# An adaLN block on one core: the transposes of the probabilities ahead of the value product

## The chip, the core and the metric

The kernel runs on one core of a Trainium2 chip. The metric is the device time of one execution, in microseconds (us). Five engines work side by side, each through its own list of instructions in order, and tell each other by semaphores when something is done: TensorE (PE in the profile, with its weight loads as PEld), VectorE (DVE), ScalarE (ACT), GpSimd (POOL) and the queue of SyncE (SP), which only starts transfers here. TensorE writes to PSUM, from where ScalarE and VectorE take its results; GpSimd works on SBUF alone.

## What is computed

A transformer block with adaptive layer norm, in float32. Two sequences of 1024 rows with 512 features; 32 query heads of 128 features share 8 key/value heads, four to one; a row attends to itself and the 127 before it. Cut to what matters:

```python
h = _layernorm(x) * (1 + ca) + sa
q, k, v = rope(h @ wq), rope(h @ wk), h @ wv
scores = jnp.einsum('bqhgd,bshd->bhgqs', qg, k) * sm_scale
allowed = (j <= i) & (j > i - SLIDING_WINDOW)
attn = jax.nn.softmax(jnp.where(allowed, scores, neg), axis=-1)
out = jnp.einsum('bhgqs,bshd->bqhgd', attn, v).reshape(B, S, N_Q_HEADS * HEAD_DIM)
x = x + ga * (out @ wo)
h = _layernorm(x) * (1 + cb) + sb
x12 = h @ w12.T + b12                       # split into x1 and x2
x = x + gb * ((silu(x1) * x2) @ w3.T + b3)
```

## The kernel before

**Units and heads.** Attention is cut into units: one key/value head with its four query heads (`G`), one tile of 128 rows of the sequence. A head has eight units, for the eight tiles of a sequence (`NT`), and there are 2 sequences with 8 heads, so 128 units. All engines walk through them in step: step u of a head starts unit u, and at the same time carries unit u-1 and unit u-2 on. The words "step 5" below mean the step that starts a head's unit 5. The loop body holds eight steps (2 to 9, where 8 and 9 are steps 0 and 1 of the next head); the first two steps and the last head of each sequence are written out behind and ahead of it by the same functions.

**Precision.** Each product is made of three matmuls (`mm3`, lines 275, 276 and 277), of the rounded part (hi) and the rest (lo) of both operands: hi by hi, hi by lo, lo by hi. So every result that TensorE consumes again is split in two: ScalarE rounds it (hi), VectorE subtracts that from the original (lo).

**The way of a unit.** `scores` (PE, 12 matmuls of 192 columns into the PSUM tile `pS`); `merge` (DVE: lines 853, 856, 859; the maximum, and `nb` from it); `exps` (ACT, line 613, into `pr`); `recip` (DVE, line 864); `normalise` (POOL, line 1193, on `pr`); then in the next step `trans` (PE, line 285: four transposes of `pr` into the PSUM tile `pTr`), `p_hi` (ACT, line 606) and `p_lo` (DVE, line 839) from `pTr` into `pT`, and `mask` (POOL, line 1186: four selects from `pT` into `pm`, two for the first unit of a head); in the step after that `p_times_v` (PE: six matmuls of 512 columns from `pm` and the values into the PSUM tile `pAv`, three for a first unit), `result_hi` (ACT, line 601) and `result_lo` (DVE, line 834) from `pAv` into `oT`, and `out_proj` (PE: 12 matmuls of 512 columns into `pOp`), which DVE adds to `y` (`add_y`, line 898). There is one `pT`, one `pm`, one `pAv` and one `oT`: `mask` of a unit waits until `p_times_v` of the unit before has read `pm`; `trans` and `p_hi` wait for the unit before too.

**What fills the rest of a step.** Between those stand the projections of the next half head ("jobs"): one or two projections in a step (12 matmuls of 512 columns each, into `pP`), with their rope: `swap` on ACT (lines 623, 624), `rope_cos` (869), `rope_sum` (875) and `rope_lo` (886) on DVE, `rope_sin` (1199) on POOL. DVE and ACT also split the weights that arrive (`split_weight`, lines 996 and 596; in steps 2, 3, 4 and 5), and in steps 4 to 6 a row tile of the other layer norm goes through ("side": `side_stats`, `side_apply` on DVE, `side_rstd` on POOL, line 1216, `side_transpose` on PE, line 383).

**What sets the order.** It is written out by hand: each engine has its own `unit_step`, which calls the functions above in one fixed order. On PE before: `scores(u)`, `p_times_v(u-2)`, `trans(u-1)`, the jobs, `out_proj(u-2)`, and what is late. On ACT: `result_hi(u-2)`, `p_hi(u-1)`, `exps(u)`, jobs. On DVE: `merge(u)`, `result_lo(u-2)`, `p_lo(u-1)`, the jobs with `recip(u)` among them, the splits, `add_y(u-2)`. On POOL: `mask(u-1)`, `normalise(u)`, the jobs' `rope_sin`, and in step 4 `side_rstd`. `mask` waits for `u_plo` of its own unit and `u_av` of the one before.

Of the kernel before, what the change touches and what calls it, by code (L numbers as in the profile page):

```python
# [71 lines left out]
def adaln_block(nc, x, wq, wk, wv, wo, w12, b12, w3, b3, cond, wmod, cos, sin, x1_spill, out):  # L72
# [13 lines left out]
    with ExitStack() as ctx:  # L86
# [114 lines left out]
        def window(a, hp):  # L201

            return 512 * a + 256 * hp
# [5 lines left out]
        def blocks(q, part):  # L209

            return q[:, part].rearrange("p h q -> p (h q)").rearrange("p (t h q) -> p t h q", t=2 * CH, h=G)
# [60 lines left out]
        def _(pe):  # L272
            def mm3(o, hi_l, lo_l, hi_r, lo_r, start, stop):

                nc.tensor.matmul(o, hi_l, hi_r, start=start, stop=False, skip_group_check=True)  # L275
                nc.tensor.matmul(o, hi_l, lo_r, start=False, stop=False, skip_group_check=True)  # L276
                return nc.tensor.matmul(o, lo_l, hi_r, start=False, stop=stop, skip_group_check=True)  # L277

            def trans(f, u):

                f.wait(u_norm, PER_U, u + 1)
                f.wait(u_phi, PER_U, u)
                f.wait(u_plo, PER_U, u)
                for i in range(G):
                    last = nc.tensor.transpose(  # L285
                        pTr[:].rearrange("p (h a q) -> p a h q", h=G, a=2)[:, i // 2, 2 * (i % 2):2 * (i % 2) + 2, :],
                        pr[:, u % 2, i, :], ident[:].rearrange("p (h q) -> p h q", h=2))
                last.then_inc(u_trans, 1)

            def scores(f, u, b):  # L290
                t = u % NT

                f.wait(j_done, PER_J, JB - 1 + (6 if t >= CH else 0) + PER_J * (u // NT))
                f.wait(u_exp, PER_U, u)
                q = qT[t // CH]
                for a in range(2):
                    lo = 0 if t else P - 64 * a
                    ks = slice(t * P - P + 64 * a + lo, t * P + 64 * a + 64)
                    for hp in range(2):
                        at = window(a, hp)  # L300
                        q_hi, q_lo = (blocks(q, i)[:, 2 * (t % CH) + a, 2 * hp:2 * hp + 2, :].rearrange(
                            "p h q -> p (h q)") for i in range(2))
                        last = mm3(pS[:, at + lo:at + 192], q_hi, q_lo, kv[:, 0, 0, ks], kv[:, 1, 0, ks], True, True)
                last.then_inc(u_scores, 1)

            def p_times_v(f, u, b):

                t = u % NT
                f.wait(u_mask, PER_U, u + 1)

                f.wait(j_done, PER_J, JB + (6 if t >= CH else 0) + PER_J * (u // NT))

                for own in ((1, 0) if t else (0,)):
                    tt = t - own
                    v_hi, v_lo = (kv[:, i, 1, tt * P:(tt + 1) * P] for i in range(2))
                    last = mm3(pAv[:], v_hi, v_lo, pm[:, own, 0].rearrange("p h q -> p (h q)"),
                               pm[:, own, 1].rearrange("p h q -> p (h q)"), own == 1 or t == 0, own == 0)
                last.then_inc(u_av, 1)
# [86 lines left out]
            def unit_step(f, u, b, jobs, late=lambda: None, prev=True, prev2=True):  # L405

                scores(f, u, b)
                if prev2:
                    p_times_v(f, u - 2, b if u >= 2 else b - 1)
                if prev:  # L410
                    trans(f, u - 1)
                jobs()
                if prev2:
                    out_proj(f, u - 2)
                late()
# [64 lines left out]
            for b in range(B):  # L480
                s0 = b * NKV
                f = Frame(pe, s0)
# [17 lines left out]
                with nc.tensor.Fori(s0, s0 + NKV - 1) as s:  # L500
                    f = Frame(pe, s, regs, s0)
                    for u in range(2, NT + 2):
                        unit_step(f, u, b, lambda: slot_jobs(f, u, b), lambda: slot_late(f, u, b))
                f = Frame(pe, s0 + NKV - 1)
# [87 lines left out]
        def _(act):  # L592
            def split_weight(f, dst, W, slot):

                f.wait(w_in[slot], 32, 16 * (W // 5 + 1))
                nc.scalar.copy(dst, st[:, slot, :]).then_inc(w_hi, 1)
# [6 lines left out]
            def p_hi(f, u):  # L603
                f.wait(u_trans, PER_U, u + 1)
                f.wait(u_mask, PER_U, u)
                nc.scalar.copy(pT[:, 0].rearrange("p h q -> p (h q)"), pTr[:]).then_inc(u_phi, 1)
# [95 lines left out]
            def splits(f, u, b):  # L702

                for k, dst in weight_pieces(u):
                    if k >= 10:
                        f.wait(j_pe, PER_J, JB + k - 10 + 1)
                    split_weight(f, dst[0], k, k % 5)

            def unit_step(f, u, b, jobs, prev=True, prev2=True, split=True):
                if u == 2:  # L710

                    f.wait(u_scores, PER_U, u + 1)
                    splits(f, u, b)
                if prev2:
                    result_hi(f, u - 2)
                if prev:
                    p_hi(f, u - 1)
                exps(f, u)
                jobs()
                if split and u in (3, 4, 5):  # L720
                    splits(f, u, b)
# [46 lines left out]
            for b in range(B):  # L768
                s0 = b * NKV
                f = Frame(act, s0)  # L770
# [12 lines left out]
                with nc.scalar.Fori(s0, s0 + NKV - 1) as s:  # L783
                    f = Frame(act, s, regs, s0)
# [4 lines left out]
                f = Frame(act, s0 + NKV - 1)  # L789
# [41 lines left out]
        def _(dve):  # L831
# [5 lines left out]
            def p_lo(f, u):  # L837
                f.wait(u_phi, PER_U, u + 1)
                nc.vector.tensor_tensor(pT[:, 1].rearrange("p h q -> p (h q)"), pTr[:],  # L839
                                        pT[:, 0].rearrange("p h q -> p (h q)"), ALU.subtract).then_inc(u_plo, 1)  # L840
# [157 lines left out]
            def splits(f, u):  # L998
                for k, dst in weight_pieces(u):
                    split_weight(f, dst, k, k % 5)  # L1000

            def unit_step(f, u, b, jobs, late=lambda: None, prev=True, prev2=True, split=True):
                merge(f, u)
                if u == 2:
                    splits(f, u)
                if prev2:
                    result_lo(f, u - 2)
                if prev:
                    p_lo(f, u - 1)
                jobs(lambda: recip(f, u))  # L1010
                if u == 4:
                    side_stats(f)
                if split and u in (3, 4, 5):
                    splits(f, u)
                if prev2:
                    b2 = b if u >= 2 else b - 1
                    add_y(f, u - 2, b2)
                if u == 4:
                    side_apply(f)
                if u == 6:  # L1020
                    side_lo(f)
                late()
# [63 lines left out]
            for b in range(B):  # L1086
                s0 = b * NKV
                f = Frame(dve, s0)
# [14 lines left out]
                with nc.vector.Fori(s0, s0 + NKV - 1) as s:  # L1103
                    f = Frame(dve, s, regs, s0)
# [3 lines left out]
                f = Frame(dve, s0 + NKV - 1)  # L1108
# [406 lines left out]
```

## Time and profile before

| | us |
|---|---|
| median of three runs | 1521.19 |
| lowest and highest of them | 1519.98, 1522.48 |
| the profiled execution, its own time | 1520.32 |
| its span, from the first to the last instruction | 1518.4 |
| TensorE busy | 1485.9 (98% of the span) |
| TensorE weight loads | 1229.1 (81%) |
| VectorE busy | 1100.7 (72%) |
| GpSimd busy | 865.4 (57%) |
| ScalarE busy | 830.5 (55%) |

A row of the timeline gives the start in us, the time taken in us, the engine, the line of the kernel, the operation, what is written and read, and how many instructions stand in the row. In brackets is idle time of the engine before it and who ended it. Matmuls overlap, so that their durations say little; the distance from one start to the next is what a matmul costs.

### The profile page before, as it was taken

What the parts mean: (1) busy time and instruction counts of PE and PEld (TensorE: products, weight loads), DVE (VectorE), ACT (ScalarE), POOL (GpSimd) and SP (SyncE); (2) the same over time, 40 slices, a digit from 0 to 9 for tenths busy, and PEclk for the clock granted to TensorE, in tenths of its full rate; (3) what the DMA queues carried; (4) which work ended last, traced back from release to release, by engine and by line L of the source; (5) the groups of instructions that cost most, each with busy time, mean ns of one, the idle gap of its engine ahead of it and who ended that gap; (6) DMA issues with size and microseconds to landing.
All of it is one profiled execution on the core that took longest, in us unless ns stands there. A gap on an engine that the chain in (4) does not pass through costs nothing.

```text
span 1518.4 us, 27309 instructions
## 1 busy us (share of the span) xinstructions
PE 1485.9 (98%) x7561; PEld 1229.1 (81%) x7561; DVE 1100.7 (72%) x1844; ACT 830.5 (55%) x2195; POOL 865.4 (57%) x892
## 2 busy tenths in 40 slices
PE   7899999999999999999999999999999999979998
PEld 3478888888888888887888888888888888868887
DVE  5578787878787878788787878787878778753542
ACT  3565565555555656655565655555556655542331
POOL 1346565656565556669855656565566656755333
PEclk9899999999999999999999999999999999989999
DMA  8111011020201111313311020111111112053001
GB/s 290 43 50 57 28 45 45 7 83 7 66 23 55 35 55 35 124 42 126 104 34 58 7 83 7 57 32 55 35 55 35 55 35 69 28 174 125 28 29 55
DMA packets 98219, 90.19 MB, mean 59 GB/s; under 512 B 5369, under 2 KB 72961, under 8 KB 98049
## 3 DMA queue, kind: packets, MB, share of 16 engines
q1 hardware_dynamic: 96464, 85.48, 17.8%
q10 hardware_dynamic: 1074, 2.11, 0.4%
q0 software_dynamic: 640, 2.10, 0.4%
q8 instruction: 20, 0.33, 0.1%
q14 instruction: 21, 0.17, 0.0%
HBM read 74.98 MB, written 14.69 MB: 59 GB/s over the span
## 4 chain that ended last, share of the span: by engine, by line
PE 84%; issue 5%; DVE 4%; POOL 3%; ACT 2%; DMA 1%; POOLq 0%; SPq 0%; ACTq 0%; DVEq 0%
PE pP L275 11%; PE pP L277 11%; PE pP L276 11%; PE pOp L275 7%; PE pOp L276 7%; PE pOp L277 7%; PE pAv L275 4%; PE pS L277 4%; PE pS L276 4%; PE pS L275 4%; PE pAv L276 4%; PE pAv L277 4%; PE pTr L285 3%; PE pXx L354 1%; DMA st<-in_L_ffn_w_dram 1%
## 5 line engine op out<-in xcount | busy, mean ns | idle before, releaser
L1186 POOL TENSOR_SCALAR_AFFINE_SELECT pm<-pT 128x512 fp32r<-128x512 f32 x480 | 393.8, 854 | 474.9 <-DVE pT L839 474.9
L275 PE MATMUL pP<-hT,wp 128*128 128x512 f32 x768 | 313.2, 408 | 1.6 <-ACT rB L624 1.6
L277 PE MATMUL pP<-hT,wp 128*128 128x512 f32 x768 | 302.3, 394 | 0.0
L276 PE MATMUL pP<-hT,wp 128*128 128x512 f32 x768 | 301.0, 392 | 0.0
L1199 POOL TENSOR_TENSOR rB<-rB,tab 128x512 f32<-128x512 f32 x160 | 218.6, 1379 | 34.1 <-ACT rB L624 34.0
L601 ACT CAST oT<-pAv 128x512 fp32r<-128x512 f32 x128 | 75.0, 586 | 281.5 <-PE pAv L277 281.5
L613 ACT ACTIVATE pr<-pS,nb 128x128 f32<-128x128 f32 x512 | 181.9, 372 | 64.0 <-DVE nb L859 63.9
L869 DVE TENSOR_TENSOR rA<-pP,tab 128x512 f32<-128x512 f32 x160 | 110.2, 689 | 137.2 <-ACT rB L624 137.2
L275 PE MATMUL pOp<-wos,oT 128*128 128x512 f32 x512 | 203.0, 397 | 4.5 <-DVE oT L834 4.2
L276 PE MATMUL pOp<-wos,oT 128*128 128x512 f32 x512 | 200.7, 392 | 0.0
L277 PE MATMUL pOp<-wos,oT 128*128 128x512 f32 x512 | 200.4, 391 | 0.0
L277 PEld LDWEIGHTS pP<-hT,wp 128*128 128x128 f32 x768 | 145.0, 189 | 32.5
L275 PEld LDWEIGHTS pP<-hT,wp 128*128 128x128 f32 x768 | 145.5, 189 | 31.8 <-issue 3.5
L276 PEld LDWEIGHTS pP<-hT,wp 128*128 128x128 f32 x768 | 145.8, 190 | 27.2
L886 DVE TENSOR_TENSOR qT<-rA,qT 128x512 fp32r<-128x512 f32 x128 | 136.0, 1081 | 19.3 <-ACT qT L633 19.3
L1193 POOL TENSOR_TENSOR pr<-pr,rs 128x512 f32<-128x512 f32 x128 | 140.0, 1094 | 7.9 <-DVE rs L864 7.9
L275 PE MATMUL pS<-kv,qT 128*128 128x192 f32 (+2 forms) x512 | 141.2, 276 | 0.5 <-DVE qT L886 0.5
L277 PE MATMUL pS<-kv,qT 128*128 128x192 f32 (+2 forms) x512 | 140.8, 275 | 0.0
L276 PE MATMUL pS<-kv,qT 128*128 128x192 f32 (+2 forms) x512 | 140.2, 274 | 0.0
L875 DVE TENSOR_TENSOR rA<-rA,rB 128x512 f32<-128x512 f32 x160 | 132.2, 858 | 3.1 <-POOL rB L1199 3.1
L623 ACT COPY rB<-pP 64x512 f32<-64x512 f32 x160 | 93.5, 584 | 68.7 <-PE pP L277 66.4
L275 PEld LDWEIGHTS pOp<-wos,oT 128*128 128x128 f32 x512 | 96.8, 189 | 31.0 <-issue 5.9
(181 smaller groups left out, 3019.7 us busy)
## 6 DMA issues: line engine op xcount, KB each, us to landing
st<-in_L_attn_wq_dram SPq DMA_DIRECT2D x64, 256.0 KB, 3.8
st<-in_L_attn_wo_dram SPq DMA_DIRECT2D x64, 256.0 KB, 3.8
h_dram<-hs SPq DMA_DIRECT2D x16, 512.0 KB
xin<-in_L_attn_x_dram SPq DMA_DIRECT2D x24, 256.0 KB, 3.2
st<-in_L_attn_wk_dram SPq DMA_DIRECT2D x16, 256.0 KB, 4.0
wm<-in_L_wmod_dram SPq DMA_DIRECT2D x4, 1024.0 KB, 8.8
st<-in_L_attn_wv_dram SPq DMA_DIRECT2D x16, 256.0 KB, 2.7
qT<-h_dram SPq DMA_DIRECT2D x2, 2048.0 KB, 11.1
```

Of the source, the lines that this page charges most:

```text
L275: nc.tensor.matmul(o, hi_l, hi_r, start=start, stop=False, skip_group_check=True)
L276: nc.tensor.matmul(o, hi_l, lo_r, start=False, stop=False, skip_group_check=True)
L277: return nc.tensor.matmul(o, lo_l, hi_r, start=False, stop=stop, skip_group_check=True)
L601: nc.scalar.copy(oT[:, 0].rearrange("p h q -> p (h q)"), pAv[:]).then_inc(u_ohi, 1)
L613: last = nc.scalar.activation(pr[:, u % 2, i, :], pS[:, at:at + P], ACT.Exp, bias=nb[:, u % 2, i:i + 1], scale=SCALE, accum_out=sums[:, u ...
L623: nc.scalar.copy(rB[0:64, r, :], pP[j % 2][64:128, :])
L869: nc.vector.tensor_tensor(rA[:, j % 3, :], pP[j % 2][:], tab[:, 0, ch * CT:(ch + 1) * CT], ALU.mult).then_inc(r_cos, 1)
L875: nc.vector.tensor_tensor(rA[:, j % 3, :], rA[:, j % 3, :], rB[:, j % 3, :], ALU.add).then_inc(r_sum, 1)
L886: nc.vector.tensor_tensor(dst, src, hi, ALU.subtract).then_inc(j_done, 1)
L1186: last = nc.gpsimd.affine_select(out=pm[:, own, part], in_=pT[:, part], compare_op=op, fill=0.0, base=0, pattern=[[0, G], [sign, P]], chan ...
L1193: nc.gpsimd.tensor_tensor(pr[:, u % 2], pr[:, u % 2], rs[:, u % 2, :].unsqueeze(2).to_broadcast([P, G, P]), ALU.mult).then_inc(u_norm, 1)
L1199: nc.gpsimd.tensor_tensor(rB[:, j % 3, :], rB[:, j % 3, :], tab[:, 1, ch * CT:(ch + 1) * CT], ALU.mult).then_inc(r_sin, 1)
```

## The change

In every step the transposes of unit u-1 and the value product of unit u-2 change places on TensorE, and the copies out of `pTr` and `pAv` change places with them on ScalarE and VectorE. Nothing is added or removed, GpSimd and SyncE keep their lists. The last units behind the loops (`p_times_v(-2)`, `trans(-1)` and so on) stay as they were.

```diff
             def unit_step(f, u, b, jobs, late=lambda: None, prev=True, prev2=True):
 
                 scores(f, u, b)
+                if prev:
+                    trans(f, u - 1)
                 if prev2:
                     p_times_v(f, u - 2, b if u >= 2 else b - 1)
-                if prev:
-                    trans(f, u - 1)
                 jobs()
...
                     splits(f, u, b)
+                if prev:
+                    p_hi(f, u - 1)
                 if prev2:
                     result_hi(f, u - 2)
-                if prev:
-                    p_hi(f, u - 1)
                 exps(f, u)
...
                     splits(f, u)
+                if prev:
+                    p_lo(f, u - 1)
                 if prev2:
                     result_lo(f, u - 2)
-                if prev:
-                    p_lo(f, u - 1)
                 jobs(lambda: recip(f, u))
```

TensorE in step 6 of the loop before, from the last matmul of the scores to the first of the projection (the registers of line 58 hold the values that the waits ahead of an operation compare with):

```order
L277 MATMUL pS<-kv,qT 128x192
L58 REGISTER_ALU x2
L275 MATMUL pAv<-pm,kv 128x512
L276 MATMUL pAv<-pm,kv 128x512
L277 MATMUL pAv<-pm,kv 128x512
L275 MATMUL pAv<-pm,kv 128x512
L276 MATMUL pAv<-pm,kv 128x512
L277 MATMUL pAv<-pm,kv 128x512
L58 REGISTER_ALU x3
L285 MATMUL pTr<-ident,pr 128x2x64 x4
L58 REGISTER_ALU x3
L275 MATMUL pP<-hT,wp 128x512
```

The same place after the change:

```order
L277 MATMUL pS<-kv,qT 128x192
L58 REGISTER_ALU x3
L285 MATMUL pTr<-ident,pr 128x2x64 x4
L58 REGISTER_ALU x2
L275 MATMUL pAv<-pm,kv 128x512
L276 MATMUL pAv<-pm,kv 128x512
L277 MATMUL pAv<-pm,kv 128x512
L275 MATMUL pAv<-pm,kv 128x512
L276 MATMUL pAv<-pm,kv 128x512
L277 MATMUL pAv<-pm,kv 128x512
L58 REGISTER_ALU x3
L275 MATMUL pP<-hT,wp 128x512
```

The four transposes, with the wait for the normalised probabilities, now follow the scores at once, and the value product stands between them and the projection.

VectorE in step 5 before, from the end of `merge`, where `oT` is the result of unit 3 and `pT` the probabilities of unit 4:

```order
L859 TENSOR_SCALAR nb<-mx 128x4
L58 REGISTER_ALU
L834 TENSOR_TENSOR oT<-pAv,oT 128x512
L58 REGISTER_ALU
L839 TENSOR_TENSOR pT<-pTr,pT 128x512
L58 REGISTER_ALU x2
L875 TENSOR_TENSOR rA<-rA,rB 128x512
```

And after the change:

```order
L859 TENSOR_SCALAR nb<-mx 128x4
L58 REGISTER_ALU
L839 TENSOR_TENSOR pT<-pTr,pT 128x512
L58 REGISTER_ALU
L834 TENSOR_TENSOR oT<-pAv,oT 128x512
L58 REGISTER_ALU x2
L875 TENSOR_TENSOR rA<-rA,rB 128x512
```

`p_lo` has moved up by one place and `result_lo` down by one. All behind them stands where it stood.

## Rows read from the trace of the kernel before

**Rows 1.** The page: busy time, share of the span and instructions of each engine.

```profile
PE 1485.9 (98%) x7561; PEld 1229.1 (81%) x7561; DVE 1100.7 (72%) x1844; ACT 830.5 (55%) x2195; POOL 865.4 (57%) x892
```

**Rows 2.** Timeline of TensorE, steps 4 to 7 of one head: where parts begin.

```profile
430.76 0.34 PE L275 MATMUL pS<-kv,qT 128*128 128x192 f32 x1
...
432.16 0.42 PE L275 MATMUL pAv<-pm,kv 128*128 128x512 f32 x1
...
442.23 0.25 PE L275 MATMUL pS<-kv,qT 128*128 128x192 f32 x1
...
448.26 0.49 PE L275 MATMUL pOp<-wos,oT 128*128 128x512 f32 x1
...
451.48 0.34 PE L275 MATMUL pS<-kv,qT 128*128 128x192 f32 x1
...
452.97 0.49 PE L275 MATMUL pAv<-pm,kv 128*128 128x512 f32 x1
...
463.08 0.25 PE L275 MATMUL pS<-kv,qT 128*128 128x192 f32 x1
```

**Rows 3.** Timeline of GpSimd over the same steps (mask 3, sines, side, mask 4, normalise 5).

```profile
438.05 2.40 POOL L1186 TENSOR_SCALAR_AFFINE_SELECT pm<-pT 128x512 fp32r<-128x512 f32 x4 [6.25 <-DVE pT L839]
...
441.41 2.53 POOL L1199 TENSOR_TENSOR rB<-rB,tab 128x512 f32<-128x512 f32 x2
443.90 1.00 POOL L1216 TENSOR_TENSOR hmv<-hmv,half 128x1 f32<-128x1 f32 x1
448.84 4.00 POOL L1186 TENSOR_SCALAR_AFFINE_SELECT pm<-pT 128x512 fp32r<-128x512 f32 x4 [3.94 <-DVE pT L839]
452.81 1.04 POOL L1193 TENSOR_TENSOR pr<-pr,rs 128x512 f32<-128x512 f32 x1
```

**Rows 4.** Timeline of VectorE there (two weight splits: the first alone, then both).

```profile
437.07 0.68 DVE L839 TENSOR_TENSOR pT<-pTr,pT 128x512 fp32r<-128x512 f32 x1
...
442.79 1.71 DVE L996 TENSOR_TENSOR wp<-st,wp 128x512 fp32r<-128x512 f32 x1
...
442.79 2.31 DVE L996 TENSOR_TENSOR wp<-st,wp 128x512 fp32r<-128x512 f32 x2
...
446.07 0.42 DVE L853 COPY_PREDICATED pS<-swapped,pS 128x256 f32<-128x256 uint8 x1
...
447.35 0.69 DVE L834 TENSOR_TENSOR oT<-pAv,oT 128x512 fp32r<-128x512 f32 x1
447.95 0.68 DVE L839 TENSOR_TENSOR pT<-pTr,pT 128x512 fp32r<-128x512 f32 x1
```

**Rows 5.** Timeline of VectorE and GpSimd where a normalise meets a `rope_lo` (step 1).

```profile
409.38 1.47 POOL L1193 TENSOR_TENSOR pr<-pr,rs 128x512 f32<-128x512 f32 x1
...
409.87 1.53 DVE L886 TENSOR_TENSOR qT<-rA,qT 128x512 fp32r<-128x512 f32 x1
```

**Rows 6.** Timeline of TensorE in step 1: scores, value product, transposes.

```profile
402.45 0.25 PE L275 MATMUL pS<-kv,qT 128*128 128x192 f32 x1
402.54 0.28 PE L276 MATMUL pS<-kv,qT 128*128 128x192 f32 x1
...
403.77 0.41 PE L275 MATMUL pAv<-pm,kv 128*128 128x512 f32 x1
404.02 0.40 PE L276 MATMUL pAv<-pm,kv 128*128 128x512 f32 x1
...
405.17 0.60 PE L285 MATMUL pTr<-ident,pr 128*128 128x128 f32 x4
```

**Rows 7.** The last step of all: timeline of VectorE and TensorE.

```profile
1363.97 0.68 DVE L834 TENSOR_TENSOR oT<-pAv,oT 128x512 fp32r<-128x512 f32 x1
...
1364.71 0.75 PE L275 MATMUL pOp<-wos,oT 128*128 128x512 f32 x1 [3.41 <-DVE oT L834]
```

**Rows 8.** Windows: width, then busy us (x instructions) of PE, PEld, DVE, ACT, POOL; clock; DMA.

```profile
1365.00:1368.00 3.00, 3.00 (x8) 2.33 (x8) 0.43 (x2) 0.61 (x4) 2.67 (x5) 0.50 0.44 79
...
442.00:463.00 21.00, 21.00 (x110) 17.51 (x109) 18.22 (x30) 12.48 (x35) 14.91 (x15) 1.00 0.00 0
```

## The prediction, made before the changed kernel had run

> **What bounds the kernel now.** I read the page first: TensorE is busy for 98% of the span, the next engine, VectorE, for 72% [rows 1], and over steps 4 to 6 of a head the granted clock is full, 1.00 [rows 8]. Matmuls overlap in the records, so "98% busy" does not say that TensorE never waits a little: small waits vanish in it. They show in the distance between starts. So next I laid the timeline of TensorE over whole steps. Steps 4 and 6 hold the same matmuls apart from what ends the step before: 12 for scores, 6 for the value product, 4 transposes, 24 for two projections, 12 for the output. Step 4 takes 442.23 - 430.76 = 11.47 us, step 6 takes 463.08 - 451.48 = 11.60 [rows 2]. In the 0.13 difference there is one cause that can be seen: the value product begins 432.16 - 430.76 = 1.40 behind the scores' start in step 4 and 452.97 - 451.48 = 1.49 in step 6, 0.13 after GpSimd's mask of unit 4 ends (448.84 + 4.00 = 452.84) [rows 2, 3]. The second small wait is in step 5: the output projection of unit 3 starts at 448.26, just 0.22 behind the end of `result_lo` of unit 3 at 447.35 + 0.69 = 448.04 [rows 2, 4]. The two recur once in each head. The rest of a head is TensorE back to back. So the time can only change by (a) what the switches between kinds of matmul cost, and (b) the few waits that TensorE meets: these two, new ones, and one longer one at the very end [rows 7].
>
> **The sum is made against the profiled execution**, 1520.32 us with a span of 1518.4; the median of the runs, 1521.19, is 0.87 above it, and I add that at the end.
>
> **Part 1: the order on TensorE by itself.** Before, a step goes scores, value product, transposes, projection. The value product's first matmul is followed 404.02 - 403.77 = 0.25 later by the second, where the next five take (405.17 - 404.02) / 5 = 0.23 each: 0.02 to 0.03 for the switch [rows 6]. After, the order is scores, transposes, value product, projection, and the open question is whether the 0.02 to 0.03 goes away. It may be only the way in which starts are recorded: the first score matmul is followed after 402.54 - 402.45 = 0.09, where the twelve average (403.77 - 402.45) / 12 = 0.11, so what is short at the entry is given back at the exit. In that case the exit to the transposes gives it back as well and the change is worth nothing. Bounds: -0.03 us a step and 0, and, as nothing in the trace shows transposes directly behind scores, +0.02 on the other side. Over some 125 steps: -3.8 to +2.5. I take -0.6, near the end that the short entry speaks for.
>
> **Part 2: the wait of step 6 goes.** VectorE is late in step 5 (`merge` starts at 446.07, 3.84 into the step), so `result_lo` and `p_lo` stand directly behind each other, 447.95 - 447.35 = 0.60 apart [rows 4]. With the order changed, `p_lo` of unit 4 takes the first place, mask 4 starts at least 0.60 earlier, and the value product wants it about 0.35 later than before, for the transposes (I put each at the 0.11 of a score matmul, 4 x 0.11 = 0.44, less the overlap of the first) stand ahead. The wait of 0.13 us is gone: 15 heads (the last one has other work there) x 0.13 = **-2.0**.
>
> **Part 3: the wait of step 5 seems to grow, but the splits come earlier.** `result_lo` of unit 3 has moved down a place, so it would end 0.60 later, at 448.64, with the output projection of unit 3 waiting for it on TensorE, and everything queued behind that. Taken alone: 15 x 0.60 = +9.0. But look at what made VectorE late. In step 4 its first weight split takes 1.71 us from 442.79 [rows 4], while both together take 2.31, so the second adds 0.60. The long one ends 0.56 after GpSimd's second sine (441.41 + 2.53 = 443.94) [rows 3]: with both its inputs in SBUF it stood until GpSimd was done. That sine hangs on GpSimd's own list: mask 3 (438.05), normalise 4, two sines without a gap. Mask 3 starts 0.30 after `p_lo` of unit 3, at 437.07 + 0.68 [rows 3, 4], and in step 4 as well VectorE is late, so `p_lo` moves up by 0.60 there. Then the sines end 0.60 earlier (443.34), the split ends about 443.9 instead of 444.50, the side's `rstd` (443.90 + 1.00 before) ends at 444.3 and does not hold up `side_apply` (some 0.45 ahead of `merge`), and `merge` starts at 445.47. The loss and the gain are the same size: `result_lo` of unit 3 ends where it ended, and the output projection waits as today. **0**, with the +9.0 as the far end.
>
> **Part 4: the transposes of unit 5 want their probabilities earlier.** They stand in step 6, behind `normalise` of unit 5, which ended at 452.81 + 1.04 = 453.85 [rows 3], 2.37 into the step. Now they are wanted at 1.40, where the value product began in step 4 [rows 2]. All else as it was, TensorE would wait 0.97. But mask 4, ahead of the normalise on GpSimd, moves up by 0.60 twice over, by parts 2 and 3: it starts near 447.64. Four selects took 4.00 us here and 2.40 in step 4 [rows 3]; the slow ones alternate with VectorE's operations. With the start at 447.64 the first stands beside `result_lo`, which reads PSUM, and goes at 0.60; the others meet the rope sums and differences as before, 1.04 each: end at 451.4. Then `normalise` meets the second `rope_lo`: 1.47 instead of 1.04 in the one place where that is seen [rows 5]. It ends near 452.8, or at 452.4 without the meeting: 1.3 or 0.9 into the step. The transposes follow a release by about 0.13, as the value product does, so they start at 1.4 to 1.5, not 0.97 late but 0 to 0.1, with about 0.1 more until weight loads run ahead again. Bounds: 0 and +0.35 (the selects all slow). I take 0.13, like the wait that it replaces: 15 x 0.13 = **+2.0**.
>
> The trace shows one side blocking the other there, to the end of its operation [rows 3, 4]. The Trainium skill, page "SBUF — State Buffer", section "Who interferes with whom", says the same as a rule: of VectorE with two SBUF inputs and a GpSimd operation that reads SBUF, the first holds the shared port for its whole length. By that rule `rope_lo`, issued first, goes ahead of the normalise and the term stays at +2.0; without it the term is 0.
>
> **Part 5: the last step.** At the end of the attention TensorE idles 3.41 us until `result_lo` of unit 5 of the last head ends at 1364.65, with `p_lo` directly behind [rows 7]. That one moves down a place: **+0.6**, once, and there is no cover for it.
>
> **What hides the rest.** The scores, `merge`, `exps` stay in place. ScalarE's pair ends when TensorE's second result is there, which is the same moment as before, so `exps` start as before. Where VectorE is not late (steps 0, 1, 3, 7) `p_lo` ends about 1.2 us earlier and so does the mask; `result_lo` ends where `p_lo` ended. `out_proj` wants it after a projection at least (12 x 0.23 = 2.7 us), which covers it everywhere but in step 5. Nothing is queued differently on GpSimd and SyncE.
>
> **Sum:** -0.6 - 2.0 + 0 + 2.0 + 0.6 = 0.0. So 1520.3 for a profiled execution and 1521.2 for the median; I say **1521.0**.
>
> **The rivals.**
> - *Slower, the splits do not come earlier* (part 3 fails): the sines wait for ScalarE's swap, or the split meets another operation. Then `result_lo` ends 0.60 later in step 5 of every head, +9.0; TensorE is then late itself and part 4 falls to 0. -0.6 - 2.0 + 9.0 + 0.6 = +7.0: 1528. It decides from a shift of the second sine under about 0.1 us. Against it: the two sines stand gapless behind the normalise. 12%.
> - *Slower, the transposes wait* (part 4 at 0.35 or over, up to 0.5 where mask 4 gains only 0.60): -0.6 - 2.0 + 15 x (0.35 to 0.5) + 0.6 = +3.3 to +5.5: 1525.5. 10%.
> - *Faster:* the switch gains its 0.03 in each step and the transposes find their probabilities: -3.8 - 2.0 + 0.6 = -5.2: 1516. For it: both waits are near their edge. 20%.
> - *The clock.* TensorE runs at its upper level, 2.4 GHz, throughout steps 4 to 6 (1.00 granted), and at the lower one (0.50) after the long idle time of the last step [rows 8]. Twelve score matmuls and four transposes in a row make no idle time, so I expect no change. The Trainium skill, page "TensorE: Matmul & The Clock Gate", section "Part 4: PE-mode transpose", says that transposes do not engage the full clock as matmuls do, which would speak against putting them next to the short scores. If it fell for 3 us in each head, 3 us would hold half the work [rows 8]: +1.5 x 15 = +22: 1543. 1%.
> - *Nothing moves at all,* since the small waits were never TensorE's: the same time as my forecast, within it.
>
> **How the numbers follow.** Forecast 57%, inside 1518.2 to 1524.2. A measurement of this kernel can tell about 0.2%, 3.0 us, from no change. Faster by more: the 20%. Slower by more: 12 + 10 + 1 = 23%. The range goes from the faster rival's 1516 to 1526, over most of the waiting transposes, and leaves out the far end of part 3 and the clock.
>
> **What would show it.** Right: step 6 without a late value product; `merge` in step 5 about 0.6 earlier relative to the scores; the first split of step 4 near 1.1 us; normalise of unit 5 ending some 1.0 earlier; the output projection of step 5 still within 0.2 to 0.3 of `result_lo`. Wrong: steps 5 longer than 9.26 (442.23 to 451.48 before [rows 2]) by 0.6, or a gap between the last score and the first transpose in steps other than 6.

## The result, and the profile after

The changed kernel is slower: 1524.71 us against 1520.12 in the runs made side by side, a ratio of 1.0032 (95% interval 1.0024 to 1.0040). The forecast was 1521.0, no change, with a range up to 1526; the time lies in the range, but the loss is real. A loss of more than 3.0 us had been given 23%, for other causes than the one found.

The page of the changed kernel. The busy times are nearly those of [rows 1]: GpSimd has 12 us less, ScalarE 5.5 more, VectorE and TensorE about the same:

```profile
span 1523.3 us, 27309 instructions
PE 1487.4 (98%) x7561; PEld 1233.0 (81%) x7561; DVE 1100.9 (72%) x1844; ACT 836.0 (55%) x2195; POOL 853.0 (56%) x892
```

So the page does not say where the loss is. What does is the length of the steps, from the first score matmul of one to that of the next. The table has their medians over the heads (in ns, from the starts in each trace):

| step | before | after | difference |
|---|---|---|---|
| 0 | 11463 | 11400 | -63 |
| 1 | 8627 | 8620 | -7 |
| 2 | 10666 | 10660 | -6 |
| 3 | 9006 | 9201 | +195 |
| 4 | 11454 | 11404 | -50 |
| 5 | 9231 | 9079 | -152 |
| 6 | 11618 | 11664 | +46 |
| 7 | 9003 | 9201 | +198 |

Between the two profiled executions the span grew by 4.9 us. Of that, the regular heads (steps 8 to 59 and 68 to 123 of the 128) hold +1.9, steps 2 to 7 +0.5, the change from the first sequence to the second (steps 60 to 67) +2.5, the three steps before the last -1.0, the last step and what follows +1.7, and the start -0.7.

**Steps 3 and 7 are the new wait.** The timeline of GpSimd, VectorE and TensorE in step 3, before:

```profile
426.79 4.00 POOL L1186 TENSOR_SCALAR_AFFINE_SELECT pm<-pT 128x512 fp32r<-128x512 f32 x4 [2.31 <-DVE pT L839]
430.76 1.04 POOL L1193 TENSOR_TENSOR pr<-pr,rs 128x512 f32<-128x512 f32 x1
...
428.23 2.07 DVE L886 TENSOR_TENSOR qT<-rA,qT 128x512 fp32r<-128x512 f32 x2
...
430.41 0.60 PE L354 MATMUL pXx<-ident,rB 128*128 128x128 f32 x4
```

and after (the step begins at 422.03, that of the kernel before at 421.76):

```profile
425.81 3.30 POOL L1186 TENSOR_SCALAR_AFFINE_SELECT pm<-pT 128x512 fp32r<-128x512 f32 x4 [1.45 <-DVE pT L839]
429.08 1.47 POOL L1193 TENSOR_TENSOR pr<-pr,rs 128x512 f32<-128x512 f32 x1
...
428.63 2.48 DVE L886 TENSOR_TENSOR qT<-rA,qT 128x512 fp32r<-128x512 f32 x2
...
430.66 0.60 PE L354 MATMUL pXx<-ident,rB 128*128 128x128 f32 x4
431.24 0.35 PE L275 MATMUL pS<-kv,qT 128*128 128x192 f32 x1
```

Before, the mask of this step started 5.03 into it and the normalise at 9.00, when the two `rope_lo` were over (430.30, 8.54 into the step). Now the mask starts at 425.81 - 422.03 = 3.78, so the normalise is issued at 7.05, in the middle of them. It takes 1.47 instead of 1.04, and the pair of `rope_lo` 2.48 instead of 2.07, to 431.11, which is 9.08 into the step. The scores of the next step read that `qT`. They start 0.13 behind its end, at 431.24, and 0.58 behind the start of the transposes of the values, where it was 430.76 - 430.41 = 0.35 before [rows 2]. (The pair also begins 0.13 later in the step, at 6.60 instead of 6.47, since the earlier mask meets the rope sums of line 875, 2.00 instead of 1.72. Experiment 1 keeps that, and there it costs nothing.)

**Steps 4 to 6**, of the same head, answer to [rows 2 to 4]. TensorE:

```profile
442.65 0.25 PE L275 MATMUL pS<-kv,qT 128*128 128x192 f32 x1
...
448.55 0.49 PE L275 MATMUL pOp<-wos,oT 128*128 128x512 f32 x1
...
451.73 0.34 PE L275 MATMUL pS<-kv,qT 128*128 128x192 f32 x1
...
453.01 0.28 PE L277 MATMUL pS<-kv,qT 128*128 128x192 f32 x1
453.35 0.65 PE L285 MATMUL pTr<-ident,pr 128*128 128x128 f32 x4
453.76 0.47 PE L275 MATMUL pAv<-pm,kv 128*128 128x512 f32 x1
...
463.41 0.25 PE L275 MATMUL pS<-kv,qT 128*128 128x192 f32 x1
```

GpSimd and VectorE:

```profile
437.70 2.40 POOL L1186 TENSOR_SCALAR_AFFINE_SELECT pm<-pT 128x512 fp32r<-128x512 f32 x4 [7.15 <-DVE pT L839]
...
441.07 2.56 POOL L1199 TENSOR_TENSOR rB<-rB,tab 128x512 f32<-128x512 f32 x2
443.57 1.02 POOL L1216 TENSOR_TENSOR hmv<-hmv,half 128x1 f32<-128x1 f32 x1
447.93 3.76 POOL L1186 TENSOR_SCALAR_AFFINE_SELECT pm<-pT 128x512 fp32r<-128x512 f32 x4 [3.35 <-DVE pT L839]
451.65 1.48 POOL L1193 TENSOR_TENSOR pr<-pr,rs 128x512 f32<-128x512 f32 x1
...
443.20 1.57 DVE L996 TENSOR_TENSOR wp<-st,wp 128x512 fp32r<-128x512 f32 x2
...
445.76 0.41 DVE L853 COPY_PREDICATED pS<-swapped,pS 128x256 f32<-128x256 uint8 x1
...
447.03 0.69 DVE L839 TENSOR_TENSOR pT<-pTr,pT 128x512 fp32r<-128x512 f32 x1
447.64 0.68 DVE L834 TENSOR_TENSOR oT<-pAv,oT 128x512 fp32r<-128x512 f32 x1
```

Mask 3 starts 437.70 - 431.24 = 6.46 into step 4 (7.29 before), the two weight splits together take 1.57 instead of 2.31, and `merge` starts 3.11 into step 5 instead of 3.84. `result_lo` 3 ends at 448.32, 5.67 into the step; before it was 5.81. In step 6 the normalise ends at 453.13, 1.40 in, and the transposes start at 1.62 (453.35): they wait.

**The last steps.** The same place as [rows 7], VectorE first, and two windows of 13 us that begin 1.7 and 1.5 us ahead of that output projection (columns as in [rows 8]), of the kernel before and the changed one:

```profile
1367.74 0.68 DVE L834 TENSOR_TENSOR oT<-pAv,oT 128x512 fp32r<-128x512 f32 x1
...
1368.47 0.79 PE L275 MATMUL pOp<-wos,oT 128*128 128x512 f32 x1 [4.01 <-DVE oT L834]
```

```profile
1363.00:1376.00 13.00, 11.29 (x45) 9.18 (x46) 4.34 (x9) 2.58 (x10) 8.35 (x11) 0.87 0.84 269
```

```profile
1367.00:1380.00 13.00, 11.53 (x41) 9.27 (x42) 3.54 (x8) 2.58 (x10) 8.38 (x11) 0.74 0.84 280
```

TensorE idles 4.01 instead of 3.41, and afterwards runs longer at its lower level: a mean clock of 0.74 against 0.87. In windows of the same length it gets 41 matmuls done instead of 45. The longer idle time alone does not decide this: the kernel of experiment 1 idles 4.02 us there and has 0.87 in such a window, with 45 matmuls, and that of experiment 4 idles 3.42 and has 0.74. What does is open. Of the 1.7 us by which the last step and what follows grew, 0.6 are the idle time and some 1.1 come with the lower clock of this execution.

### The profile page after: what moved, and what is told of

The parts are those of the page before. It is cut to its first block, busy times and chain, and to the rows that moved or that the text cites. A ratio compares the mean times of both kernels' runs of the same rounds, so it can differ in the third digit from the quotient of the medians.

```text
span 1523.3 us, 27309 instructions
## 1 busy us (share of the span) xinstructions
PE 1487.4 (98%) x7561; PEld 1233.0 (81%) x7561; DVE 1100.9 (72%) x1844; ACT 836.0 (55%) x2195; POOL 853.0 (56%) x892
## 4 chain that ended last, share of the span: by engine, by line
PE 84%; issue 6%; POOL 4%; DVE 3%; ACT 1%; DMA 1%; POOLq 0%; ACTq 0%; SPq 0%; DVEq 0%
PE pP L275 11%; PE pP L276 10%; PE pP L277 10%; PE pOp L275 7%; PE pOp L276 7%; PE pOp L277 7%; PE pS L275 4%; PE pS L277 4%; PE pS L276 4%; PE pTr L285 4%; PE pAv L275 4%; PE pAv L276 4%; PE pAv L277 3%; POOL pm L1186 1%; PE pXx L354 1%
## 5 line engine op out<-in xcount | busy, mean ns | idle before, releaser
L1186 POOL TENSOR_SCALAR_AFFINE_SELECT pm<-pT 128x512 fp32r<-128x512 f32 x480 | 365.7, 797 | 449.1 <-DVE pT L839 449.0
L275 PE MATMUL pP<-hT,wp 128*128 128x512 f32 x768 | 302.1, 393 | 1.6 <-ACT rB L624 1.6
L276 PE MATMUL pP<-hT,wp 128*128 128x512 f32 x768 | 301.4, 392 | 0.0
L277 PE MATMUL pP<-hT,wp 128*128 128x512 f32 x768 | 300.5, 391 | 0.0
L1199 POOL TENSOR_TENSOR rB<-rB,tab 128x512 f32<-128x512 f32 x160 | 215.0, 1353 | 50.8 <-ACT rB L624 50.8
L606 ACT CAST pT<-pTr 128x512 fp32r<-128x512 f32 x128 | 75.0, 586 | 185.1 <-PE pTr L285 185.1
L1193 POOL TENSOR_TENSOR pr<-pr,rs 128x512 f32<-128x512 f32 x128 | 158.9, 1241 | 27.6 <-DVE rs L864 27.6
L886 DVE TENSOR_TENSOR qT<-rA,qT 128x512 fp32r<-128x512 f32 x128 | 152.3, 1208 | 19.2 <-ACT qT L633 19.2
L875 DVE TENSOR_TENSOR rA<-rA,rB 128x512 f32<-128x512 f32 x160 | 146.1, 943 | 3.1 <-POOL rB L1199 3.1
```

Source lines behind the costliest of these rows:

```text
L875: nc.vector.tensor_tensor(rA[:, j % 3, :], rA[:, j % 3, :], rB[:, j % 3, :], ALU.add).then_inc(r_sum, 1)
L886: nc.vector.tensor_tensor(dst, src, hi, ALU.subtract).then_inc(j_done, 1)
L1186: last = nc.gpsimd.affine_select(out=pm[:, own, part], in_=pT[:, part], compare_op=op, fill=0.0, base=0, pattern=[[0, G], [sign, P]], chan ...
L1193: nc.gpsimd.tensor_tensor(pr[:, u % 2], pr[:, u % 2], rs[:, u % 2, :].unsqueeze(2).to_broadcast([P, G, P]), ALU.mult).then_inc(u_norm, 1)
L1199: nc.gpsimd.tensor_tensor(rB[:, j % 3, :], rB[:, j % 3, :], tab[:, 1, ch * CT:(ch + 1) * CT], ALU.mult).then_inc(r_sin, 1)
```

## The experiments

All ratios are to the kernel before, run on the same chip. What each does to the steps is in this table (medians in ns):

| kernel | ratio (interval) | 3 | 4 | 5 | 6 | 7 | 0 |
|---|---|---|---|---|---|---|---|
| before | 1 | 9006 | 11454 | 9231 | 11618 | 9003 | 11463 |
| changed | 1.0032 (1.0024 to 1.0040) | 9201 | 11404 | 9079 | 11664 | 9201 | 11400 |
| normalise held back in steps 3 and 7 | 1.0023 (1.0012 to 1.0033) | 8979 | 11394 | 9304 | 11636 | 8979 | 11401 |
| held back in step 7 | 1.0011 (1.0002 to 1.0020) | 9199 | 11407 | 9090 | 11651 | 8979 | 11401 |
| held back in step 3 | not timed (one execution) | 8979 | 11394 | 9297 | 11642 | 9198 | 11410 |
| old order on VectorE in steps 3 and 7 | 1.0036 (1.0022 to 1.0051) | 9108 | 11638 | 8979 | 11571 | 9105 | 11628 |
| new order in the loop bodies only | 1.0027 (1.0016 to 1.0039) | 9195 | 11412 | 9093 | 11632 | 9195 | 11404 |
| new order on TensorE only | 1.0165 (1.0149 to 1.0180) | 9104 | 11649 | 8980 | 12571 | 9104 | 11649 |
| new order on ScalarE and VectorE only | 1.0064 (1.0048 to 1.0079) | 9368 | 11452 | 9003 | 11459 | 9366 | 11458 |
| VectorE's swap in step 4 only | 0.9960 (0.9946 to 0.9975) | 9005 | 11458 | 9003 | 11459 | 9003 | 11463 |
| new order in steps 0 and 4 only | 0.9944 (0.9930 to 0.9958) | 9003 | 11390 | 8992 | 11454 | 9003 | 11357 |

**1. The normalise held back behind the last rope_lo**, on the changed kernel. It takes the meeting away and leaves every order as it is.

```diff
                     mask(f, u - 1)
+                if u % NT in (3, 7):
+                    f.wait(j_done, PER_J, JB + PER_J * (u // NT) + (5 if u % NT == 3 else 11))
                 normalise(f, u)
```

> The changed kernel with one wait more: in steps 3 and 7 GpSimd starts the normalise only when VectorE has ended the last rope_lo of the half head. Theory A (the meeting): in these two steps the normalise, which now comes earlier, meets the second rope_lo (1.52 us instead of 1.12), and the scores of the next step wait for that rope_lo. Then steps 3 and 7 go back from 9.20 us to 9.00, rope_lo to 1.12, and 30 x 0.20 = 6.0 us are won: about 1518.7, 0.4% under the changed kernel. Theory B (the order on TensorE itself, transposes behind the scores and the wait behind them): nothing changes in those steps, about 1524.7 or a little over.

Timeline of the end of step 3 (which begins at 422.56), VectorE, GpSimd and TensorE:

```profile
429.16 1.63 DVE L886 TENSOR_TENSOR qT<-rA,qT 128x512 fp32r<-128x512 f32 x2
...
430.95 1.04 POOL L1193 TENSOR_TENSOR pr<-pr,rs 128x512 f32<-128x512 f32 x1 [1.31 <-DVE qT L886]
...
431.54 0.34 PE L275 MATMUL pS<-kv,qT 128*128 128x192 f32 x1
```

The mechanism is shown: the pair takes 1.63 instead of 2.48, and both steps are down by 0.22, even below those of before. But only 0.0009 of the ratio came back where 0.004 was expected, with intervals that overlap. One reason is that step 5 grew from 9079 to 9304, as much as step 3 had lost. The sum of steps 3 to 5 (in us) is 29.69 before, 29.68 changed and 29.68 here.

**2 and 3. Held back in one of the two steps only.**

```diff
                     mask(f, u - 1)
+                if u % NT == 7:
+                    f.wait(j_done, PER_J, JB + PER_J * (u // NT) + 11)
                 normalise(f, u)
```

> The changed kernel, with the normalise held back behind the last rope_lo in step 7 only. Theory A, now with a second part: after step 3 the wait of the scores is not lost, since the output projection of step 5 waits for VectorE, whose work hangs on the transposes of the values in step 3 (from there to that projection 17.87 us in the changed kernel and 17.88 with both steps held back), so holding back pays in step 7 alone. Then step 7 lasts 8.98 instead of 9.20, steps 3, 4 and 5 stay at 9.20, 11.40 and 9.08, and 15 x 0.22 = 3.3 us are won: 0.2% under the changed kernel. Theory C (both steps pay alike and the growth of step 5 with both held back had another cause): the sum of steps 3 to 5 stays, but step 7 wins only half of what the two together won, under 1 us.

The other has `u % NT == 3` and 5 in place of 11.

> The changed kernel, with the normalise held back behind the last rope_lo in step 3 only. Theory A: step 3 falls from 9.20 to 8.98, step 5 grows from 9.08 to about 9.30, the sum of steps 3 to 5 stays at 29.68, step 7 stays at 9.20: no gain. Theory C: step 5 stays at 9.08, and the sum falls by 0.22 in each head, 3.3 us in all.

Both as theory A says. In step 3 nothing is to be won: 8979 + 11394 + 9297 = 29.67 us. In step 7 the 0.22 are, and the ratio falls from 1.0032 to 1.0011. Experiment 1 has the same gain in its steps but 1.0023 by its runs; the two intervals overlap, so the ratios put what is won anywhere from a quarter to two thirds of the loss. The traces agree with each other: in both kernels the regular heads are 3.2 us shorter than in the changed kernel, and so 1.3 to 1.4 us shorter than before the change, while steps 60 to 67 are 1.0 to 1.1 us longer than in the changed kernel (the mean granted clock from 700 to 760 us is 0.97 in both, 1.00 in the changed kernel). So the meeting is the whole loss of the regular heads, and the changed kernel's other losses stay. Why step 3 is different can be read from the chain behind it. The transposes of the values in step 3 release ScalarE and VectorE for the weight splits, these make VectorE late in step 4, its `p_lo` 3 starts mask 3, and so on to `result_lo` 3 and the output projection in step 5. From those transposes to that projection it is 448.55 - 430.66 = 17.89 us in the changed kernel (the medians over the heads are 17.88 changed, 17.80 before and 17.80 with both steps held back). When the scores in between come sooner, the projection does not.

**4. VectorE's old order in steps 3 and 7**, on the changed kernel.

```diff
-                if prev:
+                if prev and u % CH != 3:
                     p_lo(f, u - 1)
                 if prev2:
                     result_lo(f, u - 2)
+                if prev and u % CH == 3:
+                    p_lo(f, u - 1)
```

> The changed kernel, with VectorE's result_lo ahead of p_lo again in steps 3 and 7 only. Theory A: the mask starts some 0.6 us or more later there, the normalise comes after the last rope_lo, steps 3 and 7 last 9.00 us instead of 9.20: 30 x 0.20 = 6.0 us less, about 1518.7. Theory B: TensorE's order is untouched, 1524.7.

A miss for both. Steps 3 and 7 fell by half of what theory A said, and steps 0 and 4 grew. The timeline of GpSimd, and of TensorE at the end of the scores of step 4 (which begins at 429.90):

```profile
426.27 4.00 POOL L1188 TENSOR_SCALAR_AFFINE_SELECT pm<-pT 128x512 fp32r<-128x512 f32 x4 [3.15 <-DVE pT L839]
430.24 1.03 POOL L1195 TENSOR_TENSOR pr<-pr,rs 128x512 f32<-128x512 f32 x1
...
431.21 0.28 PE L277 MATMUL pS<-kv,qT 128*128 128x192 f32 x1
431.49 0.54 PE L285 MATMUL pTr<-ident,pr 128*128 128x128 f32 x3
```

The meeting is gone (the normalise takes 1.03 again), but it now ends at 431.27, 1.37 into step 4. The transposes want it there and wait: steps 4 and 0 grew by 0.23. Only half of the 0.20 came back because the old order on VectorE now waits itself: `result_lo`, first again, needs the value product, which TensorE ends later. It starts 3.98 us into the step instead of 3.53, the pair of `rope_lo` ends at 8.98 instead of 8.54 (it takes 2.07, as before), and the scores follow 0.13 behind. With the new order on TensorE the normalise of steps 3 and 7 has a window: later than the last `rope_lo` and earlier than the transposes.

**5. The new order in the loop bodies alone** (each of the three swaps under `if f.regs is not None`, the old order in the written-out steps).

> The new order on all three engines in the loop bodies alone; the first two steps and the last head of each sequence, written out, keep the old order. Theory A: what the last heads lose (steps 60 to 67 of the 128 took 2.5 us more, and steps 124, 126 and 127 0.5 each, of which a shorter wait for a transfer took back 2.0) goes: 2 to 4 us less than the changed kernel, 1521 to 1523, with steps 3 and 7 at 9.20 as before. Theory B: the loss is spread over all steps, and leaving out 20 of 128 gives back a sixth of 4.6, 0.8 us: 1524.

Steps 60 to 67 take 0.9 us more than before instead of 2.5, and from step 124 to the end the time is that of before within 0.1; the loop steps are those of the changed kernel. In the timed ratio (1.0027 against 1.0032) the difference is 0.8 us, which by itself fits theory B, and smaller than the intervals, so this part rests on one trace of each kernel. What happens in the last head of the first sequence shows in the changed kernel's waits of TensorE there (us in total, times, longest), and in its timeline:

```profile
PE pTr L285 <- POOL pr L1193: 3.7, 3, 2.0
```

```profile
698.72 0.65 PE L285 MATMUL pTr<-ident,pr 128*128 128x128 f32 x4 [1.15 <-POOL pr L1193]
```

In this head GpSimd has the residual of each tile to do as well and is late. In the kernel before, the same list has 0.8 us for the value product behind the mask, and the transposes behind the normalise are not in it.

**6. The new order on TensorE alone.** `trans(f, u - 1)` ahead of `p_times_v(f, u - 2, ...)`, ScalarE and VectorE as before.

> The new order on TensorE alone; ScalarE and VectorE take the results in the old order. Theory A (waits decide, TensorE's order by itself costs nothing): ScalarE's p_hi stands behind result_hi, which now waits for the later value product, so p_lo and the mask come 0.5 later, exps too. Where the normalise ends late the transposes wait: step 6 by 1.0 to 1.1, steps 0 and 4 by 0.2 to 0.3, and the waits of step 5 stay: 15 x 1.1 + 30 x 0.25 = +24 us, less 2.4 for the value product's old wait: about 1540. Theory B (what counts is only that transposes stand behind scores): the changed kernel's 0.3% and no more, 1524.

1.0165, or 25 us where theory A said some 20: right in kind. Step 6 and steps 0 and 4 grew as it has it; that the waits of step 5 stay was wrong (8980 against 9231), though the sum of steps 3 to 5 stayed once more (29.73 us), and steps 3 and 7 grew by 0.10 as in experiment 4. Step 6 (which begins at 453.83), GpSimd and TensorE:

```profile
455.11 1.03 POOL L1193 TENSOR_TENSOR pr<-pr,rs 128x512 f32<-128x512 f32 x1
...
455.12 0.28 PE L277 MATMUL pS<-kv,qT 128*128 128x192 f32 x1
456.37 0.65 PE L285 MATMUL pTr<-ident,pr 128*128 128x128 f32 x4 [0.97 <-POOL pr L1193]
```

This is the wait that part 4 of the prediction began with, before it took the earlier mask into account: the normalise ends 2.31 into the step, and the step takes 1.11 more than the 11459 that it takes without a wait. That both numbers are 0.97 is chance: there it ran from the place where the transposes are wanted to the end of the normalise, in the row it runs from the modelled end of the last score matmul to the start of the transposes.

**7. The new order on ScalarE and VectorE alone.** The two swaps of the diff without that of TensorE.

> The new order on ScalarE and VectorE alone; TensorE as before. ScalarE's p_hi then waits for the transposes, which come last on TensorE, and result_hi and exps come 0.5 later. Theory A: exps, the rope sums and the last rope_lo come 0.5 later in steps 3 and 7 and the scores behind them wait 0.15 to 0.2 (+5 us); in steps 5 and 6 the waits go as in the kernel with step 4 alone (-4 to -5 us); the last heads lose their 2 us. Sum about +2: 0.1 to 0.2% over the kernel before. Theory B: with TensorE's order back nothing is lost and the waits of steps 5 and 6 go: 0.3% under the kernel before.

1.0064, or 9.7 us where theory A said 2: right in kind for the steps, a miss in size. The last heads lost more than the 2 us as well: steps 60 to 67 alone take 3.5 more than before. Steps 5 and 6 lose their waits (9003 and 11459), and steps 3 and 7 grow by 0.36, not 0.15 to 0.2: the last `rope_lo` ends at 430.31, 9.25 into the step that begins at 421.06, 0.71 later than before. Here it is not longer (the pair has its 2.07); the normalise, issued behind it, bears the meeting. VectorE, GpSimd and TensorE:

```profile
428.24 2.07 DVE L886 TENSOR_TENSOR qT<-rA,qT 128x512 fp32r<-128x512 f32 x2
...
429.73 1.47 POOL L1193 TENSOR_TENSOR pr<-pr,rs 128x512 f32<-128x512 f32 x1
...
430.43 0.35 PE L275 MATMUL pS<-kv,qT 128*128 128x192 f32 x1
```

**8. VectorE's swap in step 4 only**, on the kernel before: the part of the change from which the prediction drew its gain.

```diff
+                if prev and u == 4:
+                    p_lo(f, u - 1)
                 if prev2:
                     result_lo(f, u - 2)
-                if prev:
+                if prev and u != 4:
                     p_lo(f, u - 1)
```

> The kernel before, with p_lo ahead of result_lo on VectorE in step 4 only; TensorE and ScalarE as before. Theory A: mask 3 starts 0.6 us earlier, the second sine and with it the weight split too (1.1 us instead of 1.7), merge of step 5 starts at about 3.25 instead of 3.85 into the step. So result_lo 3 and mask 4 come 0.6 earlier, and the waits of TensorE in steps 5 (0.19) and 6 (0.16) go: 15 x 0.35 = 5.2 us less than before, about 1515. Theory B: the split's length has nothing to do with the sine, then p_lo 3 earlier changes nothing that TensorE waits for: 1520, the same as before.

0.9960, and the steps are those of theory A: steps 5 and 6 fall from 9231 and 11618 to 9003 and 11459, no other moves by more than 0.004; over the regular heads that is -5.1 us and with steps 2 to 7 -5.6, where 5.2 was expected for the 15 heads. The timeline of GpSimd and VectorE in steps 4 and 5 (step 4 begins at 428.03, step 5 at 439.49):

```profile
438.08 2.55 POOL L1201 TENSOR_TENSOR rB<-rB,tab 128x512 f32<-128x512 f32 x2
...
433.74 0.69 DVE L839 TENSOR_TENSOR pT<-pTr,pT 128x512 fp32r<-128x512 f32 x1
434.34 0.68 DVE L834 TENSOR_TENSOR oT<-pAv,oT 128x512 fp32r<-128x512 f32 x1
...
440.05 1.13 DVE L996 TENSOR_TENSOR wp<-st,wp 128x512 fp32r<-128x512 f32 x1
...
442.76 0.41 DVE L853 COPY_PREDICATED pS<-swapped,pS 128x256 f32<-128x256 uint8 x1
```

The sines end at 440.63 and the first split 0.55 behind them, at 441.18; it took 1.71 in [rows 4] and takes 1.13. `merge` starts 3.27 into step 5.

**9. The new order on all three engines, in steps 0 and 4 only.**

```diff
+                new = u in (4, 8) and (f.regs is not None or b == 0)
+                if prev and new:
+                    trans(f, u - 1)
                 if prev2:
                     p_times_v(f, u - 2, b if u >= 2 else b - 1)
-                if prev:
+                if prev and not new:
                     trans(f, u - 1)
```

and the same for `p_hi`, `result_hi` and for `p_lo`, `result_lo`.

> The kernel before, with the new order on all three engines in steps 0 and 4 only (not in the first steps of a sequence nor in the very last head). Theory A (the gain is mask 3 and through it the weight split; the transposes find their probabilities, since normalises 7 and 3 end 1.04 into steps 0 and 4 and are wanted at 1.40; the meeting in steps 3 and 7 does not arise, as the order there is the old one): steps 3 and 7 stay at 9.00, step 5 falls to 9.00 and step 6 to 11.46 as with VectorE's swap in step 4 alone (-5.1 us), and steps 0 and 4 fall by 0.06 each, as they did where the normalise was held back: another -1.8 us. About 7 us or 0.45% under the kernel before. Theory D (the -0.06 was only a late start of the step before that was made up for): -5.1 us, 0.34%, with steps 0 and 4 at 11.46.

The fastest of all, 1510.56 us: 0.9944 (0.9930 to 0.9958). Against experiment 8, steps 0 and 4 are 0.11 and 0.07 shorter, and step 1 is 0.02 longer. So the -0.06 was no made-up lateness. The traces show where it stands: in both steps the projections behind the changed pair take 5.44 us from the first of them to the output projection, instead of 5.57 and 5.56, and the transposes and the value product together 0.03 and 0.05 more (medians). So it is the order on TensorE by itself that is worth something in these steps, when no wait is behind it. In all it is 8.5 us by the ratio and 7.1 in the regular heads of the trace, where theory A said 7. The intervals of experiments 8 and 9 overlap; that 9 is the faster one rests on the steps in the traces.

## Why the prediction was wrong

**The step that failed** is the paragraph "What hides the rest". It says that where VectorE is not late, in steps 0, 1, 3 and 7, `p_lo` ends 1.2 us earlier "and so does the mask", and stops there, as if earlier could only be good. It had to be followed on: the mask earlier, the normalise earlier, and in steps 3 and 7 that puts it onto the second `rope_lo`, which the next scores wait for. The price stood in [rows 5], 1.47 and 1.53 where the two meet, and part 4 used it for step 5 alone. The price was 0.20 us in most of the 27 steps 3 and 7 of the regular heads, 4.9 us counted by these steps alone. In step 3 it was no loss, since it came back in step 5; what step 7 cost is the 3.2 us by which experiments 1 and 2 shorten the regular heads.

No rival had this wait in it. The nearest, the waiting transposes with 1525.5, is near the measured time by luck: that wait costs 0.20 in step 6 (11664 against 11459 without a wait), not 0.35 or more. All five signs that the prediction named for being right came true (the value product of step 6 is not late, `merge` of step 5 0.73 earlier, the first split at 0.97, the normalise of unit 5 0.97 earlier, the output projection 0.23 behind `result_lo`), and neither sign of being wrong showed in the regular heads, for none looks at the end of steps 3 and 7. A gap between the last score and the first transpose outside step 6 came in the change of sequences alone (1.15 at 698.72).

**Part 1, the order on TensorE:** -0.6 taken, bounds -3.8 to +2.5. In steps 1 and 2 it is -0.007 each, as taken; in steps 3 and 7, without the meeting, -0.03, and in steps 0 and 4 -0.05 to -0.1. With the normalise held back, the steps without a wait (0 to 4 and 7) are 0.19 shorter in all than before, which over 15 heads is 2.8 us. The size was off, within the bounds. The part looked at the switch from the scores to the value product alone. The larger price stands behind the transposes, in step 1 before where the projection starts:

```profile
405.52 0.48 PE L275 MATMUL pP<-hT,wp 128*128 128x512 f32 x1
...
405.84 0.40 PE L276 MATMUL pP<-hT,wp 128*128 128x512 f32 x1
```

These two start 0.32 apart where others do 0.23. In the changed kernel the value product, which now follows the transposes, pays it (0.32 in the median), and the projection starts its first two 0.23 apart.

**Part 2, the wait of the value product in step 6:** right. Experiment 8 takes away the lateness of mask 4 and leaves TensorE's order, and step 6 falls by 0.16, where 0.13 was read from one head.

**Part 3, the weight split and the sine:** right, with the far end never reached. The first split fell from 1.71 to 0.97, and the output projection in step 5 waits less than before, not as long: step 5 gained 0.15 where 0 was forecast. Experiment 1 shows that this gain is step 3's own 0.2, which gave VectorE that much time: without it step 5 has 9304. The rival that the splits would not come earlier fell.

**Part 4, the transposes in step 6:** the mechanism and the numbers came as said: the normalise ended 1.40 into the step (1.3 was forecast), took 1.48 in its meeting, and the transposes started 0.22 after the 1.40 that was wanted, where 0.13 was taken for the wait. With what follows it the wait costs 0.20, so step 6 grew by 0.05, where parts 2 and 4 together said 0. The Trainium skill, page "SBUF — State Buffer", section "Who interferes with whom", says that the first of the two holds the shared port and the other is blocked. The trace agrees: `rope_lo`, started at 451.11, ended at 452.22, and the normalise, started at 451.65, took 1.48. The same rule, followed through steps 3 and 7, puts the second `rope_lo` behind the normalise, which the trace shows there as well (it ends 0.56 behind it).

**Part 5, the last step:** +0.6 was forecast and +0.6 came, but as the first of a series. Steps 124 and 126 have the same output projection right behind `result_lo` and lost 0.5 and 0.4, since the weight transposes that stand between are shorter than a projection: the cover of "a projection at least" is not there in the last head. Behind the idle time the lower clock lasted longer in this execution, which cost some 1.1 us; experiment 1 has the same idle time without that. Step 125, in which TensorE waits for a transfer of weights, was 2.0 us shorter, which paid these back; it differs between the traces of otherwise equal stretches, so it can't be counted on.

**The change of sequences** (steps 60 to 67, +2.5) is the second term that was put at nothing; it was not looked at: the prediction took one regular head and multiplied. There GpSimd is the late engine, and an operation that needs its result 1.4 us earlier waits.

**The clock rival** fell: in the changed kernel too the granted clock is 1.00 over steps 4 to 6 (from 442.60 to 463.40 in its trace), and over the whole stretch from 84.2 to 1347 us.

## What to carry to other kernels

Work that comes earlier on an engine off the critical path is not free: follow it to what it then runs beside, above all where two engines block each other, and to the operation that is queued behind that. A gain in one step must be followed to the next place where the busiest engine is tied to a late one: in this kernel 0.22 us in step 3 came to nothing and the same in step 7 was won. And when a change is made in every step, make it in each step alone in thought: here the new order in two steps of eight (0 and 4) carried the gain, that in two others (3 and 7) the loss, and the steps at the ends of the loops have other neighbours.

## What the runs showed of the hardware

In these traces a GpSimd operation on SBUF and a VectorE operation with both inputs in SBUF did not share but waited for each other in turn: the weight split ended 0.56, 0.55 us behind the end of the sine wherever that lay (444.50 against 443.94, 441.18 against 440.63), the normalise took 1.04 alone and 1.47 in a meeting, and two `rope_lo` 1.63 when the second met nothing, 2.07 beside the mask and 2.48 beside mask and normalise. VectorE's copies out of PSUM (`p_lo`, `result_lo`) took 0.67 to 0.70 in all 256 cases of the changed kernel.

TensorE's granted clock behind its longest wait differed between executions, and not by the length of the wait: over 13 us from just ahead of its end the mean was 0.74 behind 4.01 us (the changed kernel) and 0.87 behind 4.02 (experiment 1), 0.87 behind 3.41 (the kernel before) and 0.74 behind 3.42 (experiment 4). What sets it is not shown.

Behind four transposes of 128 columns, the first two matmuls of 512 columns started 0.31 to 0.32 us apart (medians of the kernels before and after), and all further ones 0.23.
